# Last stage of a four-layer kernel: rows scattered before their affine, and another order of the routing steps

## The chip, the cores and the metric

The kernel runs on one core of a Trainium2 chip. The metric is the device time of one execution in microseconds. Before the change the median of three runs was 1690.9 us (1688.8 to 1695.48).

## What is computed

Four layers follow one another on `x` (2 x 1024 rows of 256). The change touches only the last one, a mixture of eight experts between two layer norms. Cut to that:

```python
def _ln(x, g, b, eps=1e-05):
    mu = jnp.mean(x, -1, keepdims=True)
    v = jnp.mean((x - mu) ** 2, -1, keepdims=True)
    return (x - mu) * jax.lax.rsqrt(v + eps) * g + b

def _moe(x, wg, w1, b1, w2, b2):          # S = 2048 rows, E = 8, cap = 256
    gates = jax.nn.softmax(xf @ wg, axis=-1)
    idx = jnp.argmax(gates, axis=-1)
    mask1 = jax.nn.one_hot(idx, E)
    loc = jnp.sum((jnp.cumsum(mask1, 0) - 1.0) * mask1, -1)
    keep = loc < cap
    slot = jnp.where(keep, idx * cap + loc, E * cap)
    disp = jnp.zeros((E * cap, D)).at[slot].set(xf, mode='drop').reshape(E, cap, D)
    h = jnp.einsum('ecd,edf->ecf', disp, w1) + b1[:, None, :]
    y = (jnp.einsum('ecf,efd->ecd', h, w2) + b2[:, None, :]).reshape(E * cap, D)
    return jnp.where(keep[:, None], gate_val[:, None] * y[slot], 0.0)

y1 = _ln(x + _mha(x, ...), ln1_g, ln1_b)
y2 = _ln(y1 + _moe(y1, ...), ln2_g, ln2_b)
```

There is no nonlinearity between `w1` and `w2`, so the kernel uses their product (`g.w12`, 256 x 256 for each expert) and one offset row for each expert (`g.c12`).

## The kernel before, in words

The last stage is the function `tail`. Its 2048 rows are 16 tiles of 128, taken as eight pairs. Each engine has its own instruction stream, written out by hand, and semaphores tie the streams together; there is no planner. The stage has three parts.

**Routing.** For each pair p, TensorE makes the sums before the norm in PSUM (`products`). VectorE takes their statistics (`measure`), ScalarE the root (`deviation`), and VectorE writes the normalised rows (`scale`). TensorE turns these (`turn`), ScalarE applies gain and offset on the way to `y1f` (`keep_rows`), TensorE makes the eight logits (`logits`) and ScalarE copies them (`keep_logits`). VectorE picks the expert (`choose`), TensorE counts the rows ahead (`count` on TensorE) and VectorE works out the slot (`count` on VectorE). All eight pairs pass through one loop on each engine, and a step of a later kind stands at a distance: in iteration i VectorE measures pair i, chooses for pair i-3, scales pair i and counts pair i-4. PSUM has two buffers for the sums (`ps_n`); products of pair i wait until pair i-2 is scaled.

GpSimd makes the residual rows in the same loop: two tensor operations for each pair, gain and then offset, from `nrm` (two buffers) into `y1t`. From iteration 4 on it also issues the indirect DMAs that scatter the two tiles of pair i-4 from `y1t` to `slot_rows` in HBM, which SyncE has zeroed.

**Experts.** When all 16 scatters have landed, SyncE loads the slots in four pieces into `held`. For each expert TensorE turns 256 slots (`turn_slots`), ScalarE copies them to `turned`, TensorE multiplies, VectorE adds the offset row (`outputs`) and SyncE stores the result. After each copy ScalarE also makes a piece of the last residual (`outcome`).

**Gather and second norm.** GpSimd issues 16 indirect DMAs back into `held` once all results are stored. VectorE adds `y1t` and measures (`mix`), ScalarE normalises, TensorE turns, VectorE finishes (`give`), SyncE stores.

Here `then` settles after each of its operations: VectorE waits for the result before the next one starts. A line such as `dve.wait_ge(y1t_step, 2 * (p - 1))` waits on a semaphore count.

Of the kernel before, what the change touches and what calls it, by code (L numbers as in the profile page):

```python
# [13 lines left out]
ALU = mybir.AluOpType  # L14
# [2005 lines left out]
def tail(nc, a, g, out):  # L2020

    with Stage(nc, "tail") as st:
# [65 lines left out]
        def _(dve):  # L2088
# [19 lines left out]
            def scale(p):  # L2108
                dve.wait_ge(sd_done, p + 1)
                then(dve.reciprocal(sd[:, 0, 2 * p:2 * p + 2], sd[:, 0, 2 * p:2 * p + 2]))  # L2110
                if p >= 2:
                    dve.wait_ge(t_ready, p - 1)
                    dve.wait_ge(y1t_step, 2 * (p - 1))
                s.did(normalize(2 * p, nrm[p % 2][:, 0, :], ps_n[p % 2][:, 0, :]))
                normalize(2 * p + 1, nrm[p % 2][:, 1, :], ps_n[p % 2][:, 1, :]).then_inc(n_done, 1)
                dve.wait_ge(n_done, p + 1)
# [106 lines left out]
        def _(pool):  # L2223
# [10 lines left out]
            pool.wait_ge(presets, 6)  # L2234
            pool.wait_ge(spread_done, 1)
            for i in range(NPAIR + 4):
                if i < NPAIR:
                    y = y1t[:, 2 * i:2 * i + 2, :]
                    pool.wait_ge(n_done, i + 1)
                    pool.tensor_tensor(y, nrm[i % 2][:], affine[:, 0, :].unsqueeze(1).to_broadcast([P, 2, D]), ALU.mult).then_inc(y1t_step, 1)  # L2240
                    pool.wait_ge(y1t_step, 2 * i + 1)
                    pool.tensor_tensor(y, y, affine[:, 1, :].unsqueeze(1).to_broadcast([P, 2, D]), ALU.add).then_inc(y1t_step, 1)
                if i == 4:
                    pool.wait_ge(rows_written, 16 * 2)
                if i >= 4:
                    p = i - 4
                    pool.wait_ge(vstep, marks["slot", p])
                    pool.wait_ge(y1t_step, 2 * (p + 1))
                    for t in range(2 * p, 2 * p + 2):
                        pool.indirect_dma_start(g.slot_rows, bass.IndirectOffsetOnAxis(ap=slot[:, t:t + 1], axis=0),  # L2250
                                                y1t[:, t, :], None).then_inc(g.row_load[0], 16)
            pool.wait_ge(g.row_load[0], scattered)
            pool.wait_ge(vstep, marks["row"])
# [9 lines left out]
        def _(pe):  # L2263
# [12 lines left out]
            def turn(p):  # L2276
# [42 lines left out]
            def expert(e):  # L2319
                pe.wait_ge(y1f_done, NPAIR * C + e + 1)  # L2320
# [25 lines left out]
            for i in range(NPAIR + 4):  # L2346
                if i < NPAIR:
                    products(i)
                if 0 <= i - 2 < NPAIR:
                    turn(i - 2)  # L2350
                if 0 <= i - 3 < NPAIR:
                    if i == 3:
                        pe.wait_ge(spread_done, 1)
                    logits(i - 3)
                if 0 <= i - 4 < NPAIR:
                    count(i - 4)
# [10 lines left out]
        def _(act):  # L2367
# [221 lines left out]
```

## Time and profile before

| | us |
|---|---|
| median of three runs | 1690.9 |
| the profiled execution | 1689.8 |
| its span | 1688.1 |
| TensorE busy | 1504.5 |
| VectorE busy | 1080.0 |
| ScalarE busy | 446.1 |
| GpSimd busy | 462.6 |
| mean granted TensorE clock | 0.94 of full speed |

The span runs from the first to the last instruction of one execution; start and end around it take the other 1.7 us. The last stage begins at about 1554 us and takes the last 134 us. PE is TensorE, DVE is VectorE, ACT is ScalarE, POOL is GpSimd, and SPq is the queue of SyncE. A busy TensorE is not necessarily a TensorE at its peak, since the ends of pipelined matmuls are modelled.

### The profile page before, as it was taken

What the parts mean: (1) busy time and instruction counts of PE and PEld (TensorE: products, weight loads), DVE (VectorE), ACT (ScalarE), POOL (GpSimd) and SP (SyncE); (2) the same over time, 40 slices, a digit from 0 to 9 for tenths busy, and PEclk for the clock granted to TensorE, in tenths of its full rate; (3) what the DMA queues carried; (4) which work ended last, traced back from release to release, by engine and by line L of the source; (5) the groups of instructions that cost most, each with busy time, mean ns of one, the idle gap of its engine ahead of it and who ended that gap; (6) DMA issues with size and microseconds to landing.
All of it is one profiled execution on the core that took longest, in us unless ns stands there. A gap on an engine that the chain in (4) does not pass through costs nothing. (4 is left out here: it accounts for less than half of the span.)

```text
span 1688.1 us, 26682 instructions
## 1 busy us (share of the span) xinstructions
PE 1504.5 (89%) x10586; PEld 924.9 (55%) x10586; DVE 1080.0 (64%) x3225; ACT 446.1 (26%) x687; POOL 462.6 (27%) x392
## 2 busy tenths in 40 slices
PE   7989789999999996898888889899998999698882
PEld 3447678888888884443333333344444558344761
DVE  1539898687877662487785667644783498423745
ACT  2332111111111000232333323321112477413232
POOL 0002323231415405066666575400000000000623
PEclk9999899999999997899999899999999999899865
DMA  8900000000000016365557664420142027000235
GB/s 355 228 9 1 2 2 8 2 9 2 9 2 9 3 32 224 141 196 165 172 164 266 192 208 142 131 112 1 37 163 63 14 83 240 0 7 1 70 124 107
DMA packets 86991, 155.92 MB, mean 92 GB/s; under 512 B 42075, under 2 KB 56532, under 8 KB 84308
## 3 DMA queue, kind: packets, MB, share of 16 engines
q1 hardware_dynamic: 64852, 82.91, 14.9%
q0 software_dynamic: 22016, 71.32, 14.2%
q8 instruction: 83, 1.36, 0.3%
q14 instruction: 40, 0.33, 0.1%
HBM read 141.62 MB, written 16.78 MB: 94 GB/s over the span
## 5 line engine op out<-in xcount | busy, mean ns | idle before, releaser
L514 PE MATMUL peer_ps_h<-all_x,layer_down 128*128 128x256 f32 x768 | 180.0, 388 | 0.0
L650 POOL TENSOR_TENSOR peer_bm<-peer_bm,peer_slots 128x512 f32<-128x512 f32 x36 | 109.0, 3028 | 244.7 <-DVE peer_bm L746 244.7
L1420 PE MATMUL skills_acc<-skills_hid,skills_w 128*128 128x512 f32 x256 | 129.7, 632 | 37.0 <-DVE skills_hid L1153 26.7
L514 PEld LDWEIGHTS peer_ps_h<-all_x,layer_down 128*128 128x128 f32 x768 | 144.3, 192 | 21.7 <-issue 1.9
L553 PE MATMUL peer_ps_o<-peer_hg,layer_up 128*128 128x256 f32 x640 | 142.3, 380 | 0.4 <-DVE peer_hg L778 0.4
L553 PEld LDWEIGHTS peer_ps_o<-peer_hg,layer_up 128*128 128x128 f32 x640 | 120.5, 190 | 20.4 <-issue 3.3
L595 ACT ACTIVATE peer_hg<-peer_ps_h 128x512 f32<-128x512 f32 x96 | 57.3, 597 | 274.6 <-PE peer_ps_h L514 274.6
L1473 PE MATMUL skills_ps_g<-all_x,skills_w 128*128 128x512 f32 x256 | 121.7, 598 | 0.0
L1473 PE MATMUL skills_ps_u<-all_x,skills_w 128*128 128x512 f32 x256 | 120.3, 592 | 0.0
L1420 PEld LDWEIGHTS skills_acc<-skills_hid,skills_w 128*128 128x128 f32 x256 | 50.2, 200 | 104.9 <-issue 65.0
L1487 ACT ACTIVATE skills_act_g<-skills_ps_g 128x512 f32<-128x512 f32 x96 | 56.3, 597 | 194.1 <-PE skills_ps_g L1473 170.3
L810 POOL DMA_INDIRECT layer_qw<-expert_rows,all_route x88 | 88.3, 1004 | 64.1 <-DVE layers_y L1231 37.1
L1153 DVE SCALAR_TENSOR_TENSOR skills_hid<-skills_ps_u,all_pair_w,skills_act_g 128x512 f32<-128x512 f32 x64 | 48.0, 750 | 84.2 <-ACT skills_act_g L1487 30.3
L778 DVE TENSOR_TENSOR peer_hg<-peer_ps_w,peer_hg 128x1024 f32<-128x1024 f32 x48 | 58.7, 1222 | 61.7 <-PE peer_ps_w L529 61.6
L810 POOL DMA_INDIRECT layer_w<-expert_rows,all_route x88 | 86.7, 985 | 37.8 <-issue 27.4
L810 POOL DMA_INDIRECT four_ring<-expert_rows,all_route x80 | 79.7, 996 | 51.9 <-issue 26.2
L650 POOL TENSOR_TENSOR all_route<-all_route,peer_slots 128x512 f32<-128x512 f32 x12 | 36.3, 3028 | 189.6 <-DVE all_route L746 189.6
L529 PE MATMUL peer_ps_w<-peer_bm,peer_am 64*64 64x32 f32 x4608 | 77.9, 224 | 9.1 <-DVE peer_hg L778 7.6
L1719 PE MATMUL quant_ps_m<-layers_y,layer_qw 128*128 128x512 f32 x192 | 84.1, 593 | 2.0 <-DVE layers_y L1626 2.0
L529 PEld LDWEIGHTS peer_ps_w<-peer_bm,peer_am 64*64 64x64 f32 x4608 | 73.9, 139 | 21.2 <-issue 21.2
L1473 PEld LDWEIGHTS skills_ps_g<-all_x,skills_w 128*128 128x128 f32 x256 | 49.5, 194 | 62.4 <-issue 62.4
L748 DVE TENSOR_TENSOR peer_am<-all_iota_a,peer_slots 128x2048 f32<-128x2048 f32 x36 | 82.2, 2284 | 0.0
(426 smaller groups left out, 2610.1 us busy)
## 6 DMA issues: line engine op xcount, KB each, us to landing
four_ring<-in_l_w SPq DMA_DIRECT2D x8, 1024.0 KB, 4.9
quant_w<-in_l_w SPq DMA_DIRECT2D x32, 256.0 KB, 4.6
all_early<-in_l_w SPq DMA_DIRECT2D x26, 256.0 KB, 3.8
four_skill<-in_skills SPq DMA_DIRECT2D x2, 3072.0 KB
skills_w<-in_skills SPq DMA_DIRECT2D x2, 3072.0 KB
layer_down<-in_down SPq DMA_DIRECT2D x1, 4096.0 KB, 25.5
layer_up<-in_up SPq DMA_DIRECT2D x1, 4096.0 KB, 35.2
expert_rows<-in_up SPq DMA_DIRECT2D x1, 4096.0 KB, 41.2
```

The costliest lines, as they stand in the source:

```text
L514: mm = pe.matmul(ps_h[group % 2][:, r, :], down[:, c, j * P:(j + 1) * P], g.x[:, c, bass.ds(i * PB, PB)], start=(c == 0), stop=(c == C - 1))
L529: mm = pe.matmul(ps_w[of, z, m, :], am[c % RING][token, m, of], bm[c % RING][token, m, :], start=True, stop=True)
L553: mm = pe.matmul(ps_o[:, c, :], up[:, j, c * P:(c + 1) * P], hg[half][:, j, :], start=(j == 0), stop=(j == NJ - 1))
L595: act.activation(hg[half][:, 2 * group:2 * group + 2, :], ps_h[group % 2][:], ACT.Gelu).then_inc(gelu_done, 1)
L650: pool.tensor_tensor(bm[c % RING][:], bm[c % RING][:], slots[half][:, 2, c * PAIRS:(c + 1) * PAIRS].unsqueeze(2).to_broadcast([P, PAIRS, WJ]),
L748: dve.tensor_tensor(am[c % RING][:], g.iota_a[:].unsqueeze(1).to_broadcast([P, PAIRS, P]), slots[half][:, 0, col].unsqueeze(2).to_broadcas ...
L778: dve.tensor_tensor(acts, ps_w[:].rearrange("p z m j -> p z j m"), acts, ALU.mult).then_inc(p_done, 1)
L810: pool.indirect_dma_start(to[:, k, :], None, g.table, bass.IndirectOffsetOnAxis(ap=g.eid[:, n // per, at:at + 1], axis=0)).then_inc(g.row_ ...
L1420: mm = pe.matmul(acc[q % 2][c][:], w_down[s][:, m, c * P:(c + 1) * P], hid[j % 4][:], start=(s == 0 and m == 0), stop=(s == 2 and m == M2 ...
L1473: mm = pe.matmul(bank[:], weight[:, c, m * P:(m + 1) * P], g.x[:, c, q * BLK:(q + 1) * BLK], start=(c == 0), stop=(c == C - 1))
L1487: act.activation(act_g[j % 2][:], ps_g[j % 2][:], ACT.Gelu_apprx_tanh).then_inc(gelu_done, 1)
L1719: mm = pe.matmul(ps_m[n % n_ring][:], wt[z][:, c, m * P:(m + 1) * P], g.y[:, c, q * BLK:(q + 1) * BLK], start=(c == 0), stop=(c == C - 1))
```

## The change

Four things are changed, all in `tail`.

- VectorE writes the normalised rows straight into `y1t`. TensorE turns them from there, and GpSimd scatters them from there without gain and offset.
- Gain and offset are applied later and twice. On the turned slots, ScalarE does it with two half-size activations in place of one copy. On the residual rows, GpSimd does it with the same 16 tensor operations, which now stand behind the 16 scatters.
- `mix` waits for the residual rows.
- The loop is one iteration shorter. The distances are 1, 2 and 3 in place of 2, 3 and 4, and the order within an iteration is another on VectorE, TensorE and ScalarE.

```diff
-                if p >= 2:
-                    dve.wait_ge(t_ready, p - 1)
-                    dve.wait_ge(y1t_step, 2 * (p - 1))
-                s.did(normalize(2 * p, nrm[p % 2][:, 0, :], ps_n[p % 2][:, 0, :]))
+                s.did(normalize(2 * p, y1t[:, 2 * p, :], ps_n[p % 2][:, 0, :]))
...
             def mix(p):
                 dve.wait_ge(g.row_load[p % NRING], landed(p))
+                dve.wait_ge(y1t_step, 2 * (p + 1))
...
-            for i in range(NPAIR + 4):
+            for i in range(NPAIR + 3):
                 if i < NPAIR:
                     measure(i)
+                if 0 <= i - 2 < NPAIR:
+                    choose(i - 2)
+                if i == 3:
+                    dve.wait_ge(presets, 5)
                 if 0 <= i - 3 < NPAIR:
-                    choose(i - 3)
+                    count(i - 3)
                 if i < NPAIR:
                     scale(i)
-                if i == 4:
-                    dve.wait_ge(presets, 5)
-                if 0 <= i - 4 < NPAIR:
-                    count(i - 4)
...
             pool.wait_ge(presets, 6)
+            pool.wait_ge(rows_written, 16 * 2)
+            for p in range(NPAIR):
+                pool.wait_ge(n_done, p + 1)
+                pool.wait_ge(vstep, marks["slot", p])
+                for t in range(2 * p, 2 * p + 2):
+                    pool.indirect_dma_start(g.slot_rows, ...y1t[:, t, :], None).then_inc(g.row_load[0], 16)
             pool.wait_ge(spread_done, 1)
...
+            pool.wait_ge(t_ready, NPAIR)
             pool.wait_ge(g.row_load[0], scattered)
+            for p in range(NPAIR):
+                y = y1t[:, 2 * p:2 * p + 2, :]
+                pool.tensor_tensor(y, y, affine[:, 0, :]..., ALU.mult).then_inc(y1t_step, 1)
+                pool.wait_ge(y1t_step, 2 * p + 1)
+                pool.tensor_tensor(y, y, affine[:, 1, :]..., ALU.add).then_inc(y1t_step, 1)
...
-            for i in range(NPAIR + 3):
+            for i in range(NPAIR + 2):
                 if i % 2 == 0 and i // 2 + 1 < NBLK:
                     residual(i // 2 + 1)
+                if 0 <= i - 2 < NPAIR:
+                    keep_logits(i - 2)
                 if i < NPAIR:
                     deviation(i)
-                if 0 <= i - 2 < NPAIR:
-                    keep_rows(i - 2)
-                if 0 <= i - 3 < NPAIR:
-                    keep_logits(i - 3)
+                if 0 <= i - 1 < NPAIR:
+                    keep_rows(i - 1)
...
-                act.activation(turned[e % 2][:], ps_t[e % 2][:], ACT.Copy).then_inc(y1f_done, 1)
+                for c in range(C):
+                    act.activation(turned[e % 2][:, c, :], ps_t[e % 2][:, c, :], ACT.Identity,
+                                   bias=..., scale=...).then_inc(y1f_done, 1)
```

One full iteration of VectorE's routing loop, in the kernel before (`tail_g` are the largest logits, `tail_ps_n` the sums, `tail_spot` and `tail_slot` the slot numbers):

```order
L2099 BN_STATS tail_stat<-tail_ps_n 128x6 x2
L2102 BN_AGGR tail_mv<-tail_stat 128x2 x2
L2121 MAX tail_g<-tail_logit 128x8 x2
L2122 MAX_INDEX tail_gi<-tail_g,tail_logit 128x8 x2
L2123 CAST tail_gif<-tail_gi 128x2
L2124 TENSOR_TENSOR tail_hot<-all_iota_a,tail_gif 128x16
L2110 RECIPROCAL tail_sd<-tail_sd 128x2
L2106 TENSOR_SCALAR tail_nrm<-tail_ps_n,tail_mv,tail_sd 128x256 x2
L2131 TENSOR_TENSOR tail_before<-tail_free,tail_before 128x8 x2
L2133 TENSOR_TENSOR tail_keep<-tail_free,tail_before 128x16
```

The same iteration in the changed kernel, from the end of choosing to the scaled rows:

```order
L2121 TENSOR_TENSOR tail_hot<-all_iota_a,tail_gif 128x16
L2128 TENSOR_TENSOR tail_before<-tail_free,tail_before 128x8 x2
L2130 TENSOR_TENSOR tail_keep<-tail_free,tail_before 128x16
L2132 SCALAR_TENSOR_TENSOR tail_hot<-tail_keep,tail_hot 128x16
L2134 TENSOR_TENSOR tail_spot<-tail_keep,tail_spot 128x16
L2135 TENSOR_TENSOR tail_spot<-tail_spot,tail_hot 128x16
L2136 TENSOR_REDUCE tail_slot_f<-tail_spot 128x2
L2137 TENSOR_TENSOR tail_slot_f<-tail_slot_f,tail_own 128x2
L2138 CAST tail_slot<-tail_slot_f 128x2
L2110 RECIPROCAL tail_sd<-tail_sd 128x2
L2106 TENSOR_SCALAR tail_y1t<-tail_ps_n,tail_mv,tail_sd 128x256 x2
```

The slot arithmetic has moved in front of the reciprocal and the scaling, and it belongs to a pair one iteration younger.

GpSimd's stream where it meets the scatters, before:

```order
L2240 TENSOR_TENSOR tail_y1t<-tail_nrm,tail_affine 128x512
L2242 TENSOR_TENSOR tail_y1t<-tail_y1t,tail_affine 128x512
L2250 DMA slot_rows<-tail_y1t,tail_slot 4096x256 x2
L2240 TENSOR_TENSOR tail_y1t<-tail_nrm,tail_affine 128x512
L2242 TENSOR_TENSOR tail_y1t<-tail_y1t,tail_affine 128x512
L2250 DMA slot_rows<-tail_y1t,tail_slot 4096x256 x10
L2259 DMA tail_held<-out_rows,tail_row 128x256 x16
```

and in the changed kernel (the two tensor operations repeat eight times):

```order
L2231 MEMSET tail_held 128x4096
L2238 DMA slot_rows<-tail_y1t,tail_slot 4096x256 x16
L2245 TENSOR_TENSOR tail_y1t<-tail_y1t,tail_affine 128x512
L2247 TENSOR_TENSOR tail_y1t<-tail_y1t,tail_affine 128x512
L2245 TENSOR_TENSOR tail_y1t<-tail_y1t,tail_affine 128x512
```

All 16 tensor operations have moved from the routing loop to the stretch between the last scatter and the first gather.

## Rows read from the trace of the kernel before

**Rows 1.** The page's first line.

```profile
span 1688.1 us, 26682 instructions
```

**Rows 2.** The chain that ended last, by time: start us, us, what.

```profile
1620.81 3.81 DMA tail_held<-slot_rows
...
1624.67 1.97 PE tail_ps_t L2316 x8
...
1649.00 0.99 POOL tail_held L2259
```

**Rows 3.** Timeline of VectorE, routing: start us, us, instruction [idle before <-releaser].

```profile
1566.67 0.76 DVE L2099 BATCH_NORM_STATS2 tail_stat<-tail_ps_n 128x6 f32<-128x256 f32 x2 [0.42 <-PE tail_ps_n L2273]
...
1575.04 0.76 DVE L2099 BATCH_NORM_STATS2 tail_stat<-tail_ps_n 128x6 f32<-128x256 f32 x2
...
1582.83 0.76 DVE L2099 BATCH_NORM_STATS2 tail_stat<-tail_ps_n 128x6 f32<-128x256 f32 x2
...
1585.21 0.24 DVE L2121 MAX8 tail_g<-tail_logit 128x8 f32<-128x8 f32 x2 [1.34 <-ACT tail_logit L2390]
...
1587.56 0.37 DVE L2131 TENSOR_TENSOR tail_before<-tail_free,tail_before 128x8 f32<-128x8 f32 x2
...
1589.03 1.22 DVE L2138 TENSOR_TENSOR tail_spot<-tail_spot,tail_hot 128x16 f32<-128x16 f32 x1
...
1590.76 0.75 DVE L2099 BATCH_NORM_STATS2 tail_stat<-tail_ps_n 128x6 f32<-128x256 f32 x2
...
1606.32 0.23 DVE L2121 MAX8 tail_g<-tail_logit 128x8 f32<-128x8 f32 x2
...
1609.90 0.36 DVE L2131 TENSOR_TENSOR tail_before<-tail_free,tail_before 128x8 f32<-128x8 f32 x2
...
1611.49 0.23 DVE L2121 MAX8 tail_g<-tail_logit 128x8 f32<-128x8 f32 x2
...
1616.63 0.17 DVE L2141 CAST tail_slot<-tail_slot_f 128x2 uint32<-128x2 f32 x1 [0.76 <-DVE tail_slot_f L2140]
```

**Rows 4.** Timeline of ScalarE, one routing iteration and the first slot copy.

```profile
1583.90 0.29 ACT L2379 ACTIVATE tail_sd<-tail_mv,all_eps 128x2 f32<-128x2 f32 x1 [6.51 <-DVE tail_mv L2102]
1584.10 1.00 ACT L2385 ACTIVATE tail_y1f<-tail_ps_t,layer_cols 128x256 f32<-128x256 f32 x2
...
1625.82 0.60 ACT L2413 ACTIVATE tail_o<-tail_ps_t 128x512 f32<-128x512 f32 x1 [4.27 <-PE tail_ps_t L2316]
```

**Rows 5.** Timeline of GpSimd: one pair's residual rows, and the last scatter.

```profile
1587.61 1.26 POOL L2240 TENSOR_TENSOR tail_y1t<-tail_nrm,tail_affine 128x512 f32<-128x512 f32 x1 [1.38 <-DVE tail_nrm L2106]
1588.95 1.26 POOL L2242 TENSOR_TENSOR tail_y1t<-tail_y1t,tail_affine 128x512 f32<-128x512 f32 x1
...
1618.34 0.96 POOL L2250 DMA_INDIRECT slot_rows<-tail_y1t,tail_slot  x1 [0.30 <-issue]
```

**Rows 6.** Timeline of TensorE, routing.

```profile
1575.15 1.10 PE L2271 MATMUL tail_ps_n<-layer_w_out,layer_o 128*128 128x256 f32 x4
...
1577.84 0.60 PE L2282 MATMUL tail_ps_t<-all_ident,tail_nrm 128*128 128x128 f32 x4
...
1587.67 2.04 PE L2271 MATMUL tail_ps_n<-layer_w_out,layer_o 128*128 128x256 f32 x4 [0.16 <-DVE tail_nrm L2106]
...
1592.92 0.79 PE L2282 MATMUL tail_ps_t<-all_ident,tail_nrm 128*128 128x128 f32 x4
...
1600.86 1.88 PE L2291 MATMUL tail_free<-layer_wg,tail_y1f 128*128 128x8 f32 x8 [4.85 <-ACT tail_y1f L2385]
```

**Rows 7.** Windows: stretch, us, busy PE, PEld, DVE, ACT, POOL; clock, DMA share, GB/s.

```profile
1575.00:1578.00 3.00, 3.00 (x21) 2.79 (x21) 1.55 (x10) 1.28 (x4) 2.54 (x2) 1.00 0.01 3
...
1587.00:1590.00 3.00, 2.84 (x10) 2.40 (x10) 2.83 (x8) 0.00 (x0) 2.31 (x2) 0.50 0.08 23
```

**Rows 8.** Groups of instructions: busy us, mean ns | idle before, releasers.

```profile
L2158 DVE TENSOR_TENSOR tail_y1f<-tail_ps_n,tail_c_rows 128x512 f32<-128x512 f32 x8 | 5.5, 692 | 22.2 <-PE tail_ps_n L2327 22.2
...
L650 POOL TENSOR_TENSOR peer_bm<-peer_bm,peer_slots 128x512 f32<-128x512 f32 x36 | 109.0, 3028 | 244.7 <-DVE peer_bm L746 244.7
```

More of the change, by code:

```diff
@@ L2110, in scale @@
                 then(dve.reciprocal(sd[:, 0, 2 * p:2 * p + 2], sd[:, 0, 2 * p:2 * p + 2]))
-                if p >= 2:
-                    dve.wait_ge(t_ready, p - 1)
-                    dve.wait_ge(y1t_step, 2 * (p - 1))
-                s.did(normalize(2 * p, nrm[p % 2][:, 0, :], ps_n[p % 2][:, 0, :]))
-                normalize(2 * p + 1, nrm[p % 2][:, 1, :], ps_n[p % 2][:, 1, :]).then_inc(n_done, 1)
+                s.did(normalize(2 * p, y1t[:, 2 * p, :], ps_n[p % 2][:, 0, :]))
+                normalize(2 * p + 1, y1t[:, 2 * p + 1, :], ps_n[p % 2][:, 1, :]).then_inc(n_done, 1)
                 dve.wait_ge(n_done, p + 1)
@@ L2234, in _ @@
             pool.wait_ge(presets, 6)
-            pool.wait_ge(spread_done, 1)
[L2236 to L2251, printed above, removed]
-            pool.wait_ge(g.row_load[0], scattered)
+            pool.wait_ge(rows_written, 16 * 2)
[3 more added lines that the diff above has]
+                for t in range(2 * p, 2 * p + 2):
+                    pool.indirect_dma_start(g.slot_rows, bass.IndirectOffsetOnAxis(ap=slot[:, t:t + 1], axis=0),
+                                            y1t[:, t, :], None).then_inc(g.row_load[0], 16)
+            pool.wait_ge(spread_done, 1)
+            pool.wait_ge(t_ready, NPAIR)
+            pool.wait_ge(g.row_load[0], scattered)
+            for p in range(NPAIR):
+                y = y1t[:, 2 * p:2 * p + 2, :]
+                pool.tensor_tensor(y, y, affine[:, 0, :].unsqueeze(1).to_broadcast([P, 2, D]), ALU.mult).then_inc(y1t_step, 1)
+                pool.wait_ge(y1t_step, 2 * p + 1)
+                pool.tensor_tensor(y, y, affine[:, 1, :].unsqueeze(1).to_broadcast([P, 2, D]), ALU.add).then_inc(y1t_step, 1)
             pool.wait_ge(vstep, marks["row"])
@@ L2281, in turn @@
                     for i in range(2):
-                        mm = pe.transpose(ps_t[p % 2][:, c, i * P:(i + 1) * P], nrm[p % 2][:, i, c * P:(c + 1) * P], g.ident[:])
+                        mm = pe.transpose(ps_t[p % 2][:, c, i * P:(i + 1) * P], y1t[:, 2 * p + i, c * P:(c + 1) * P], g.ident[:])
                 mm.then_inc(t_ready, 1)
@@ L2319, in expert @@
             def expert(e):
-                pe.wait_ge(y1f_done, NPAIR * C + e + 1)
+                pe.wait_ge(y1f_done, (NPAIR + e + 1) * C)
                 if e < 2:
@@ L2345, in _ @@
             mm.then_inc(spread, 1)
-            for i in range(NPAIR + 4):
+            for i in range(NPAIR + 3):
                 if i < NPAIR:
@@ L2349, in _ @@
                 if 0 <= i - 2 < NPAIR:
-                    turn(i - 2)
+                    if i == 2:
+                        pe.wait_ge(spread_done, 1)
+                    logits(i - 2)
                 if 0 <= i - 3 < NPAIR:
[L2352 to L2356, printed above, removed]
+                    count(i - 3)
+                if 0 <= i - 1 < NPAIR:
+                    turn(i - 1)
             spread_offsets()
@@ L2412, in _ @@
                     act.wait_ge(n_ready, NPAIR + e - 1)
-                act.activation(turned[e % 2][:], ps_t[e % 2][:], ACT.Copy).then_inc(y1f_done, 1)
+                for c in range(C):
+                    act.activation(turned[e % 2][:, c, :], ps_t[e % 2][:, c, :], ACT.Identity,
+                                   bias=g.cols[:, 2 * C + c:2 * C + c + 1], scale=g.cols[:, C + c:C + c + 1]).then_inc(y1f_done, 1)
                 outcome(e // C, e % C)
```

3 lines of the change are left out of this document (2 added, 1 removed).

## The prediction, made before the changed kernel was run

> **What bounds the kernel now.** The first line of the page gives a span of 1688.1 us [rows 1]; the profiled execution took 1689.8 us, so 1.7 us lie around it, and it stands 1.1 us under the median of the three runs. Only the last stage changes, so what is ahead of it is left as it is, and I read the chain of waits of that stage next. The reader is to see two hinges there. SyncE loads the slots at 1620.81, the instant the last scatter has landed, and the next link is TensorE at 1624.67; GpSimd's first gather starts at 1649.00 [rows 2]. Everything before 1620.81 is one question: what makes the last scatter late? The 28.2 us between the hinges and the 39 us behind the second are a fixed train in which each step waits for the one before.
>
> For the first question I read VectorE's timeline in the routing loop. Iterations start at 1575.04, 1582.83, 1590.76, and the last full one ends at 1606.32; from there only choosing and counting remain, until the last slot number is written at 1616.63 + 0.17 = 1616.80 [rows 3]. The last scatter follows at 1618.34 [rows 5]. So VectorE sets the pace: four iterations take 1606.32 - 1575.04 = 31.28 us, 7.8 each. Two things inside such an iteration are not work. VectorE is idle 1.34 us before it can choose, released by the copied logits [rows 3]: ScalarE first waits for the statistics that VectorE has just made (1583.90), then keeps rows for 1.00 us from 1584.10, and only then copies logits that have long been ready [rows 4]. And the slot arithmetic takes 1590.76 - 1587.56 = 3.20 us here, while the same eight steps later take 1611.49 - 1609.90 = 1.59 us; one of its operations on 128x16 elements took 1.22 us from 1589.03 and ended at 1590.25 [rows 3], when GpSimd's tensor operation from 1588.95 ended, at 1590.21 [rows 5]. VectorE's small operation stood still behind GpSimd's.
>
> The Trainium skill, "SBUF — State Buffer", section "SBUF: two separate sides", says that a VectorE operation with two SBUF inputs and a GpSimd operation that reads SBUF exclude each other for the whole instruction. The row agrees.
>
> **The change, part by part.**
>
> *An iteration of VectorE.* Measuring takes 1583.90 - 1582.83 = 1.07 us, choosing and scaling together 1587.56 - 1585.21 = 2.35, counting without GpSimd beside it 1.59 [rows 3, 4]: 5.0 us in place of 7.8. The idle 1.34 goes because ScalarE now copies logits ahead of the deviation, provided that they are ready. TensorE's work for one iteration at full clock is one turn, the products (1577.84 - 1575.15 = 2.7 us [rows 6]), logits and count, by the rows about 0.5 + 2.7 + 0.9 + 0.5 = 4.6 us, under 5.0. Followed from the scaling of a pair: turn 0.5, rows kept after the next deviation at +1.3 to +2.3, products of a later pair until +3.2, logits until +4.1, copied at +4.3. VectorE asks for them at 5.0 + 1.07 = +6.1. So 1.8 us are to spare and 5.0 holds.
>
> *Start of the loop.* The third pair is measured at 1566.67 before [rows 3]. Now the first turn (0.4 to 0.5 us) stands ahead of its products, so it is 1567.1. Then come measure, choose and scale (3.4 us), 1570.5; the next products end 0.5 us after that, and a full iteration of 5.0 ends at 1576.1. Before, this point was at 1575.04: 1.0 us lost, since choosing and counting begin one iteration earlier.
>
> *Four full iterations.* 31.28 against 4 x 5.0 = 20.0: 11.3 us gained.
>
> *Drain.* Before, 1616.80 - 1606.32 = 10.5 us. Now choose and count (2.7), then the last pair. Its turn, kept rows, logits and copy follow the last scaling: with TensorE at half clock about 1.0 + 1.1 + 1.9 + 0.2 = 4.2 us (1.88 for the logits in [rows 6]), so that VectorE waits until +4.2, chooses (1.1), and counts twice (3.2): 8.4 us. Gain 2.1. At full clock it would be about 7.0. I take half clock, since TensorE has no products left there and the rows of the drain before show it.
>
> *Scatters.* GpSimd now only issues them, one in 0.30 + 0.96 = 1.26 us [rows 5], 2.5 for a pair, less than an iteration. Only in the drain are two pairs ready 1.6 us apart: 0.9 us lost. Landing behind the last one is as before. Taking the normalise from `nrm` to `y1t` costs nothing, as shape, source and engine stay, and the two waits in it go. The last scatter has landed 1.0 - 11.3 - 2.1 + 0.9 = 11.5 us earlier, at 1609.3. What is late next is the offset products on TensorE, which stand behind the last count (about 1602.4) and ahead of the turned slots: sixteen of 256 columns at 2.04 / 4 = 0.5 us each [rows 6] end before 1610.6, and the slots arrive at 1609.3 + 3.8 = 1613.1. Still hidden.
>
> *Turned slots.* One copy of 0.60 us becomes two halves of 1.00 us together [rows 4]. Later experts have a whole matmul of the previous expert as cover. The first has none: 0.4 us lost.
>
> *Residual rows.* Sixteen GpSimd operations at 1588.95 - 1587.61 = 1.34 us [rows 5] are 21.4 us. They start when the scatters have landed, and the gathers queue behind them on GpSimd, 28.2 us later [rows 2]. They are hidden with 6.8 us to spare. VectorE works beside them only on `outputs`, eight of 0.69 us with one operand in PSUM [rows 8]. If each of these held GpSimd up in full it would be 5.5 us more, 26.9 in all, still hidden; from the other side it is nothing. I take nothing, since VectorE's operation on PSUM at 1587.56 took 0.37 us beside GpSimd's at 1587.61 and 0.36 at 1609.90 with none [rows 3, 5]. The added wait in `mix` is then met long before. By the skill's rule, too, an operation with one SBUF input takes no lock.
>
> *Sum.* 11.5 - 0.4 = 11.1 us gained. 1689.8 - 11.1 = 1678.7; from the median it is 1679.8. I say 1679.3.
>
> **Rivals.**
>
> *A: the clock falls inside the loop and TensorE becomes the bound.* At 1575 to 1578 TensorE is busy without a break and the granted clock is 1.00 (2.4 GHz); at 1587 to 1590 it is 0.50 (1.2 GHz) [rows 7], after the waits that VectorE's slow iterations gave it. There the products took 1592.92 - 1587.67 = 5.25 us and logits 1.88 [rows 6]; with a turn of 1.0 and counts of 1.0 an iteration costs TensorE 9.1 us. For it: the new loop leaves TensorE some 10% idle in small waits. Against it: before it stood idle far more when the clock fell, and the shorter loop takes these waits away. Each iteration caught costs 9.1 - 5.0 = 4.1, the first 1.8 less. With two caught it is 6.4 us: 1679.3 + 6.4 = 1685.7. The Trainium skill, "TensorE: Matmul & The Clock Gate", section "HAM oscillation — how this bites in real kernels", warns that a matmul loop with a wait in each turn can fall back to half rate every time; the rows show one such fall.
>
> *B: GpSimd's sixteen operations outlast the experts, and the kernel gets slower.* Another 128x512 operation of GpSimd took 3.03 us on average [rows 8]. At that price they take 16 x 3.1 = 49.6 us, the gathers start 49.6 - 28.2 - 0.4 = 21.0 us late, and the time is 1679.3 + 21.0 = 1700.3. It decides from (28.2 + 0.4) / 16 = 1.8 us each. Against it: the 3.03 are taken beside large VectorE operations on SBUF alone, and no such operation runs between the hinges. The same length on the same tiles was 1.26.
>
> *C: the earlier routing is given back.* Something not seen in the rows, such as late slot loads or a colder clock at the experts, holds the second hinge. The clock there is 0.50 at the start in both kernels, and TensorE pauses for the slots in both. If three experts more ran at half clock, some 2 us each, it would cost 6 us: 1685.3.
>
> **How the numbers follow.** Forecast 0.74, A 0.13, B 0.04, C 0.09. A measurement of this kernel tells about 0.5% from no change, 8.5 us. Below 1682.4 lie the forecast and a part of A with one iteration caught: faster 0.78. The rest of A and C: same 0.17. B, and A through five iterations (which would cost 18.7), make slower 0.05. The low end is the drain at full clock (1.4 us better), no loss at the start (1.0) and some scatter of the median: 1675.5. The high end is A with two iterations: 1685.7.
>
> **What would show it.** VectorE's iterations start 5.0 us apart and L2135, the former L2138, takes 0.17 us. No idle time before the largest logits but for the last pair. The granted clock stays 1.00 up to the last products. SyncE's slot load starts at about 1609, the first gather at about 1638. GpSimd's sixteen operations end about 7 us before that gather. The forecast is wrong if iterations are longer than 6 us, or if the first gather follows directly on GpSimd's last tensor operation.

## The result, and the profile after

The changed kernel ran in 1681.15 us (median of six runs, 1676.21 to 1682.39), the kernel before in 1689.97 us in the same comparison (six runs, 1686.9 to 1695.48). The ratio is 0.9933, with a 95% interval of 0.9915 to 0.9952. The prediction said 1679.3 us, or 0.9931 of the 1690.9 us known then. In a later comparison, on a chip where everything is 4% shorter, the same two kernels gave 0.9925 (0.9911 to 0.9939).

The page and one line of VectorE's timeline (start us, duration us, instruction) give the length of the last stage. I take it from VectorE's `memset` of the counters to the end of the span. Of the changed kernel:

```profile
span 1680.7 us, 26688 instructions
```

```profile
1559.47 0.07 DVE L2197 MEMSET tail_before<- 128x8 f32 x1
```

The same line of the kernel before, which the rows above did not hold:

```profile
1555.31 0.07 DVE L2199 MEMSET tail_before<- 128x8 f32 x1
```

So the stage was 1688.1 - 1555.31 = 132.8 us long [rows 1] and is 1680.7 - 1559.47 = 121.2 us: 11.6 us shorter. The span fell by only 7.4 us, since this execution came to the stage 4.2 us later, though nothing ahead of it differs. The stage is the better ruler for what follows: its start varied by 16 us over the profiles below that are near 1690 us long, while the length of the changed kernel's stage repeated within 0.5 us.

VectorE's timeline of the changed kernel, one full iteration, the next one's start, and the drain:

```profile
1580.13 0.76 DVE L2099 BATCH_NORM_STATS2 tail_stat<-tail_ps_n 128x6 f32<-128x256 f32 x2
...
1584.85 0.76 DVE L2099 BATCH_NORM_STATS2 tail_stat<-tail_ps_n 128x6 f32<-128x256 f32 x2
1585.65 0.25 DVE L2102 BATCH_NORM_AGGREGATE tail_mv<-tail_stat 128x2 f32<-128x6 f32 x2
1585.81 0.21 DVE L2118 MAX8 tail_g<-tail_logit 128x8 f32<-128x8 f32 x2
...
1587.69 0.17 DVE L2135 TENSOR_TENSOR tail_spot<-tail_spot,tail_hot 128x16 f32<-128x16 f32 x1
...
1599.10 0.24 DVE L2118 MAX8 tail_g<-tail_logit 128x8 f32<-128x8 f32 x2
...
1603.48 0.24 DVE L2118 MAX8 tail_g<-tail_logit 128x8 f32<-128x8 f32 x2 [1.69 <-ACT tail_logit L2385]
...
1607.54 0.27 DVE L2138 CAST tail_slot<-tail_slot_f 128x2 uint32<-128x2 f32 x1
```

An iteration takes 1584.85 - 1580.13 = 4.7 us, where it was 7.8 [rows 3]. The largest logits follow the statistics without a pause, and L2135, the operation that stood at 1.22 us, takes 0.17. The one wait left is 1.69 us for the logits of the last pair. ScalarE has copied the logits in time, here by 1585.00, when VectorE asks for them at 1585.81:

```profile
1584.82 0.18 ACT L2385 ACTIVATE tail_logit<-tail_free 128x16 f32<-128x16 f32 x1 [2.39 <-PE tail_free L2286]
```

GpSimd's timeline and SyncE's load, with the second hinge:

```profile
1606.88 0.95 POOL L2238 DMA_INDIRECT slot_rows<-tail_y1t,tail_slot  x1 [2.12 <-DVE tail_hot L2132]
1608.14 0.96 POOL L2238 DMA_INDIRECT slot_rows<-tail_y1t,tail_slot  x1 [0.30 <-DVE tail_row_f L2145]
1609.41 0.96 POOL L2238 DMA_INDIRECT slot_rows<-tail_y1t,tail_slot  x1 [0.30 <-issue]
1610.67 0.96 POOL L2238 DMA_INDIRECT slot_rows<-tail_y1t,tail_slot  x1 [0.30 <-issue]
1613.24 1.26 POOL L2245 TENSOR_TENSOR tail_y1t<-tail_y1t,tail_affine 128x512 f32<-128x512 f32 x1 [1.61 <-DMA slot_rows<-tail_y1t,tail_slot]
...
1632.60 1.28 POOL L2247 TENSOR_TENSOR tail_y1t<-tail_y1t,tail_affine 128x512 f32<-128x512 f32 x1
1640.98 1.02 POOL L2254 DMA_INDIRECT tail_held<-out_rows,tail_row  x1 [7.10 <-DMA out_rows<-tail_y1f]
```

```profile
1613.14 2.02 SPq L2435 DMA_DIRECT2D tail_held<-slot_rows  x4
```

The sixteen tensor operations end at 1633.88, and GpSimd is then idle for 7.10 us until the last result has landed. That is the cover that the residual rows have. The first gather starts at 1640.98, was 1649.00 [rows 2]; against the start of the stage it comes 12.2 us earlier.

### The profile page after: what moved, and what is told of

Same layout as the page of the kernel before. It is cut to its first block and busy times, and to the rows that moved or that the text cites. A ratio compares the mean times of both kernels' runs of the same rounds, so it can differ in the third digit from the quotient of the medians.

```text
span 1680.7 us, 26688 instructions
## 1 busy us (share of the span) xinstructions
PE 1502.3 (89%) x10586; PEld 920.4 (55%) x10586; DVE 1072.3 (64%) x3225; ACT 450.2 (27%) x695; POOL 462.2 (27%) x392
## 5 line engine op out<-in xcount | busy, mean ns | idle before, releaser
L553 PEld LDWEIGHTS peer_ps_o<-peer_hg,layer_up 128*128 128x128 f32 x640 | 120.5, 190 | 20.3 <-issue 3.3
L595 ACT ACTIVATE peer_hg<-peer_ps_h 128x512 f32<-128x512 f32 x96 | 57.3, 597 | 273.8 <-PE peer_ps_h L514 273.8
L1473 PE MATMUL skills_ps_u<-all_x,skills_w 128*128 128x512 f32 x256 | 120.3, 592 | 0.0
L778 DVE TENSOR_TENSOR peer_hg<-peer_ps_w,peer_hg 128x1024 f32<-128x1024 f32 x48 | 58.7, 1223 | 62.4 <-PE peer_ps_w L529 62.3
L529 PE MATMUL peer_ps_w<-peer_bm,peer_am 64*64 64x32 f32 x4608 | 78.2, 224 | 11.1 <-DVE peer_hg L778 9.3
L1473 PEld LDWEIGHTS skills_ps_u<-all_x,skills_w 128*128 128x128 f32 x256 | 48.7, 190 | 61.8 <-issue 61.3
## 6 DMA issues: line engine op xcount, KB each, us to landing
skills_w<-in_skills SPq DMA_DIRECT2D x2, 3072.0 KB, 10.5
```

The lines of the kernel that those rows point to most:

```text
L529: mm = pe.matmul(ps_w[of, z, m, :], am[c % RING][token, m, of], bm[c % RING][token, m, :], start=True, stop=True)
L553: mm = pe.matmul(ps_o[:, c, :], up[:, j, c * P:(c + 1) * P], hg[half][:, j, :], start=(j == 0), stop=(j == NJ - 1))
L595: act.activation(hg[half][:, 2 * group:2 * group + 2, :], ps_h[group % 2][:], ACT.Gelu).then_inc(gelu_done, 1)
L778: dve.tensor_tensor(acts, ps_w[:].rearrange("p z m j -> p z j m"), acts, ALU.mult).then_inc(p_done, 1)
L1473: mm = pe.matmul(bank[:], weight[:, c, m * P:(m + 1) * P], g.x[:, c, q * BLK:(q + 1) * BLK], start=(c == 0), stop=(c == C - 1))
```

## The experiments

Twelve more profiles follow, one of them of the changed kernel again: the first four on one chip, the next four on another, the last four on a third. Six of them (logits last, plain copy, no residual affine, 16 more on GpSimd, idle matmuls, wide offsets) have one execution each, so for those only the stage in the profile is read. In the table the times are us from the start of the stage in the profiled execution. "Iteration 4" is the start of the fifth statistics, with which the full iterations begin; "pace" is the mean of the last three steps from one start of statistics to the next.

| kernel | iteration 4 | pace | slots ready | slot load | first turn | first gather | length |
|---|---|---|---|---|---|---|---|
| before | 19.7 | 7.8 | 61.5 | 65.5 | 69.4 | 93.7 | 132.8 |
| changed | 20.7 | 4.7 | 48.3 | 53.7 | 57.6 | 81.5 | 121.2 |
| deferral only | 19.3 | 6.2 | 55.5 | 60.0 | 63.9 | 88.2 | 128.1 |
| order only | 21.8 | 5.7 | 53.4 | 58.7 | 62.6 | 85.4 | 125.2 |
| changed, logits copied last | 22.4 | 6.2 | 56.4 | 61.7 | 65.6 | 90.6 | 130.2 |
| changed, one plain copy | 20.6 | 4.7 | 48.3 | 53.7 | 57.5 | 81.4 | 121.3 |
| changed, no residual affine | 20.3 | 4.7 | 48.0 | 53.4 | 57.3 | 81.0 | 120.7 |
| changed, 16 more on GpSimd | 20.6 | 4.7 | 48.3 | 53.7 | 57.5 | 94.3 | 134.4 |
| changed, drain reordered | 20.3 | 4.7 | 47.6 | 52.1 | 56.0 | 80.7 | 120.5 |
| changed, idle matmuls | 20.6 | 4.7 | 48.3 | 53.7 | 57.5 | 80.3 | 120.3 |
| changed, run again | 20.3 | 4.7 | 48.0 | 53.3 | 57.3 | 81.1 | 120.7 |
| drain and idle matmuls | 20.3 | 4.7 | 47.6 | 52.1 | 56.0 | 80.5 | 120.6 |
| changed, wide offsets | 20.4 | 4.7 | 48.1 | 53.4 | 57.3 | 81.1 | 120.9 |
| all three | 20.3 | 4.7 | 47.6 | 52.1 | 55.9 | 79.8 | 119.7 |

There are two kinds of start, 5.6 to 5.7 or 5.9 to 6.0 us until the first statistics. They go with the clock of the first products: in the last us before the stage the granted clock was 1.00 for the early kind (1554 to 1555 us in the kernel before) and 0.50 for the late kind (1558 to 1559 us in the changed kernel). The late kind shifts everything behind by 0.3 to 0.4 us. A length is best compared with the changed kernel of the same start: 121.2 for the late kind, 120.7 for the early one. The kernel before had the early start and the first profile of the changed kernel the late one, so like for like the change is worth 132.8 - 120.7 = 12.1 us in the stage.

### Deferral alone

```diff
 kernel before, and in it:
-  normalize(...) -> nrm; GpSimd makes y1t in the loop
+  normalize(...) -> y1t; GpSimd scatters raw rows, makes the residual rows behind the scatters
-  ACT.Copy of the turned slots
+  two ACT.Identity with scale and bias
   order and distances of the routing steps: as before
```

> The kernel before with only the deferral: rows scattered raw, gain and offset later, loop order and distances as before. Length of the last stage means from VectorE's memset of `before` to the end of the span: 132.8 us before (1555.3 to 1688.1), 121.2 changed (1559.5 to 1680.7). Theory 1 (two separate costs in an iteration: 1.6 us of VectorE standing behind GpSimd's tensor operations, and 1.34 us idle for the logits): iterations become 7.8 - 1.5 = 6.3 us, the idle 1.34 stays, stage 127 to 128. Rival (the order of the steps is what counts, the stalls are absorbed by waiting): iterations stay at 7.5 or more, stage 132 or more.

Ratio to the kernel before 0.9957 (0.9929 to 0.9985). The stage is 128.1 us long, the pace 6.2 us. VectorE's timeline shows that the idle time stayed and the stalls went:

```profile
1589.27 0.24 DVE L2118 MAX8 tail_g<-tail_logit 128x8 f32<-128x8 f32 x2 [1.35 <-ACT tail_logit L2385]
...
1592.38 0.18 DVE L2135 TENSOR_TENSOR tail_spot<-tail_spot,tail_hot 128x16 f32<-128x16 f32 x1
```

The first theory holds: standing behind GpSimd's operations was a cost of its own, 1.6 us in each iteration.

### Order alone

```diff
 changed kernel, and in it:
-  normalize(...) -> y1t; residual rows behind the scatters
+  normalize(...) -> nrm; GpSimd makes y1t of pair i and scatters pair i - 3 in one loop
-  two ACT.Identity on the turned slots
+  ACT.Copy
   order and distances of the routing steps: new
```

> The kernel before with only the new order and distances; GpSimd still makes the residual rows in the loop, and the copies are plain. Theory 1: the idle 1.34 goes, the stalls behind GpSimd stay, iterations 6.3 us, stage 127 to 128, so that this and the deferral alone add up to about 11.6. Rival (either edit alone gives nearly all): stage under 124. Second rival: GpSimd is the bound with two tensor operations and two scatters for a pair (5.1 us), which would show as VectorE waiting on it.

Ratio 0.9968 (0.9943 to 0.9992); the interval overlaps that of the deferral alone, and only the stage, read from one profile each, tells them apart. It is 125.2 us long, 2 us shorter than expected, at a pace of 5.7 in place of 6.3. VectorE's timeline, and GpSimd's beside it:

```profile
1590.27 0.16 DVE L2122 FIND_INDEX8 tail_gi<-tail_g,tail_logit 128x8 uint32<-128x8 f32 x1
1590.46 1.08 DVE L2123 CAST tail_gif<-tail_gi 128x2 f32<-128x2 uint32 x1
...
1592.57 0.17 DVE L2138 TENSOR_TENSOR tail_spot<-tail_spot,tail_hot 128x16 f32<-128x16 f32 x1
```

```profile
1590.25 1.27 POOL L2242 TENSOR_TENSOR tail_y1t<-tail_y1t,tail_affine 128x512 f32<-128x512 f32 x1
```

The stall is there, but only one of 0.9 us in an iteration: the cast ends at 1591.54, GpSimd's operation at 1591.52. In the other order the slot arithmetic falls between GpSimd's operations. So what GpSimd's presence costs depends on what VectorE is about to do when one of its operations starts, and the expectation of 1.6 us was carried over without asking that. The second rival is out: VectorE waited for GpSimd nowhere in the loop. The edits apart save 4.7 and 7.6 us, which adds to 12.3, and together they save 11.6 (each against the 132.8 before, all with the late start): nearly additive, and neither gives all. The ratios of whole executions stand in the other order, within their intervals.

### The logits' place on ScalarE

```diff
 changed kernel, ScalarE's loop:
-  keep_logits(i - 2); deviation(i); keep_rows(i - 1)
+  deviation(i); keep_rows(i - 1); keep_logits(i - 2)
```

> The changed kernel with one edit: ScalarE copies the logits last in its iteration, behind deviation and kept rows. Theory 1: VectorE is idle about 1.34 us in each full iteration again, iterations 4.75 + 1.3 = 6.1 us, stage longer by 6 to 8 us (127 to 129). Rival (the idle time went because the iteration has other work to fill it): stage within 1 us of 121.2.

The stage is 130.2 us long, 9.5 more than the changed kernel of the same start and over the 6 to 8 expected. The slots are ready 8.4 us later; another 1.2 us lies between first turn and first gather, where the first expert took 3.78 us, wholly at half clock. The pace is 6.2 us, and VectorE is idle for the logits again:

```profile
1588.45 0.24 DVE L2118 MAX8 tail_g<-tail_logit 128x8 f32<-128x8 f32 x2 [1.35 <-ACT tail_logit L2385]
```

ScalarE's timeline is that of the kernel before [rows 4] again, with the logits at the end:

```profile
1587.14 0.30 ACT L2374 ACTIVATE tail_sd<-tail_mv,all_eps 128x2 f32<-128x2 f32 x1 [4.89 <-DVE tail_mv L2102]
1587.34 1.00 ACT L2380 ACTIVATE tail_y1f<-tail_ps_t,layer_cols 128x256 f32<-128x256 f32 x2
1588.24 0.18 ACT L2385 ACTIVATE tail_logit<-tail_free 128x16 f32<-128x16 f32 x1
```

One copy of 0.18 us, placed behind 1.2 us of other work, costs more than the deferral gains. With it the shorter distances are worth nothing: the stage is even 2 us longer than with the deferral alone.

### The copy of the turned slots

```diff
 changed kernel:
-  for c in range(C): act.activation(turned[e % 2][:, c, :], ps_t[e % 2][:, c, :], ACT.Identity, bias=..., scale=...)
+  act.activation(turned[e % 2][:], ps_t[e % 2][:], ACT.Copy)
```

> The changed kernel with one copy of the turned slots in place of two activations; gain and offset of the expert's input are left out. Theory 1: only the first expert lacks cover, so the stage is 0.4 us shorter (120.8). Rival: each expert pays, 8 x 0.4 = 3.2 us shorter.

The stage is 121.3 us, against 121.2. The later experts are hidden, so the rival is out. The length does not show the 0.4 us of the first expert, but TensorE's timeline does, changed kernel first and plain copy second:

```profile
1617.04 1.97 PE L2311 MATMUL tail_ps_t<-all_ident,tail_held 128*128 128x128 f32 x8 [4.30 <-DMA tail_held<-slot_rows]
1619.27 3.23 PE L2322 MATMUL tail_ps_n<-layer_w,tail_o 128*128 128x256 f32 x8 [0.26 <-ACT tail_o L2409]
```

```profile
1609.39 1.97 PE L2311 MATMUL tail_ps_t<-all_ident,tail_held 128*128 128x128 f32 x8 [4.25 <-DMA tail_held<-slot_rows]
1611.20 3.46 PE L2322 MATMUL tail_ps_n<-layer_w,tail_o 128*128 128x256 f32 x8
```

From the first turn to the first expert it is 2.23 us with the halves and 1.81 with the plain copy: the 0.4 us are paid. But in both kernels the clock rose at the same time, in the 1 us windows that start 62.0 us behind the start of the stage (mean clock 0.83 and 0.85). The expert that began 0.4 us later had less of its work at half clock and was 0.23 us shorter, and by the first gather 0.1 us was left.

### Residual rows left out, and doubled

```diff
 changed kernel, behind the scatters:
-  8 x (mult by gain, add offset) on y1t         (left out)
 or
+  16 x mult on scratch, ahead of them           (doubled)
```

> The changed kernel without the sixteen tensor operations of GpSimd behind the scatters; gain and offset of the residual rows are left out. Theory 1 (hidden, with about 7 us to spare, and nothing else slowed by them): stage 121.2, within 0.3. Rival (they slow VectorE or the loads beside them): 1 us or more shorter, to be seen between slot load and first gather.

> The changed kernel with sixteen more tensor operations of the same size on GpSimd, on scratch, ahead of the sixteen. Theory 1: 16 x 1.28 = 20.5 us more against 7.1 us to spare; the first gather comes 13.4 us later and the stage is 134.6, slower than the kernel before. Rival B of the prediction (GpSimd slows itself beside VectorE's outputs): the operations are longer than 1.28 us and the stage over 136.

Without them the stage is 120.7 us, as the changed kernel of the same start. Slot load to first gather took 27.6 us against 27.8: they slow nothing beside them. With sixteen more it is 134.4 us, 0.2 from the expectation. GpSimd's timeline of the doubled kernel:

```profile
1615.44 19.70 POOL L2249 TENSOR_TENSOR tail_nrm<-tail_nrm,tail_affine 128x512 f32<-128x512 f32 x16 [1.60 <-DMA slot_rows<-tail_y1t,tail_slot]
...
1654.52 1.26 POOL L2255 TENSOR_TENSOR tail_y1t<-tail_y1t,tail_affine 128x512 f32<-128x512 f32 x1
1655.93 1.02 POOL L2262 DMA_INDIRECT tail_held<-out_rows,tail_row  x1 [0.15 <-issue]
```

The first gather now follows directly on the last tensor operation. They took 1.23 us (19.70 / 16) and 1.26 us each, those beside VectorE's outputs too, not 3.03 [rows 8]: rival B's mechanism does not occur here, but its arithmetic (time beyond the cover is paid in full) does. The 36 operations of rows 8 all lie between 3.025 and 3.031 us, which speaks for a cost of their own form and not for waiting; no run tests that.

### The drain

```diff
 changed kernel, iteration 9:
-  TensorE: logits(7), count(6)     VectorE: choose(7), count(6)
+  TensorE: count(6), logits(7)     VectorE: count(6), choose(7)
```

> The changed kernel with another order in the drain only: the count of pair 6 goes ahead of the last pair's logits on TensorE and ahead of its choosing on VectorE. The 1.69 us in which VectorE is idle for the last logits then hold a count. Slot 6 is ready 2.7 us earlier, so that GpSimd's last four scatters are no longer bunched: last scatter issued 1.9 us earlier, stage 119.3. Rival (the last pair's chain decides, the bunching is absorbed): 0.7 us or less.

The slot load comes 1.2 us earlier than in the changed kernel of the same start, the first gather 0.4 and the end 0.2 (120.5 against 120.7). In the run, the ratio to the kernel before is 0.9932 (0.9915 to 0.9948), no different from the changed kernel. The bunching did go (the last pair's scatters start 0.75 us after its slots are written), but most of the gain was lost behind the load. TensorE's timeline:

```profile
1613.63 1.97 PE L2313 MATMUL tail_ps_t<-all_ident,tail_held 128*128 128x128 f32 x8 [3.00 <-DMA tail_held<-slot_rows]
1615.85 3.78 PE L2324 MATMUL tail_ps_n<-layer_w,tail_o 128*128 128x256 f32 x8 [0.26 <-ACT tail_o L2413]
```

The first expert took 3.78 us at half clock, where that of the changed kernel took 3.15 with the same start and 3.23 with the late one. The first turns began 1.3 us earlier, but the clock did not rise earlier. Windows of 1 us, 61 us behind the start of the stage, of the changed kernel of the same start and of this one:

```profile
1547.47:1548.47 1.00, 1.00 (x4) 0.82 (x3) 0.00 (x0) 0.57 (x1) 1.00 (x2) 0.56 0.01 4
```

```profile
1618.67:1619.67 1.00, 1.00 (x5) 0.71 (x4) 0.00 (x0) 0.00 (x0) 0.92 (x2) 0.51 0.00 0
```

In the window before, the clock is 0.50 in both, in the one behind 1.00. So most of the time won ahead of the experts was spent at half clock in the first of them.

### The clock ahead of the experts

Four kernels followed that up. Idle matmuls are matmuls whose result nobody reads:

```diff
             spread_offsets()
+            pe.wait_ge(vstep, marks["counted", NPAIR - 1])
+            for n in range(4):
+                pe.matmul(free[2][:, 0:D], g.ident[:], g.w12[:, 0, n % E3, :], start=True, stop=True)
             turn_slots(0)
```

> The changed kernel with four matmuls of 128x256 into unused PSUM, in TensorE's pause of 4.3 us before the turned slots. At half clock they take 1.0 us each, so they fit. Theory: the granted clock answers to work on all 128 rows, so it rises earlier; the first turns take 0.9 in place of 2.0 us and the first expert 1.7 in place of 3.2; the stage is 1.5 to 2.6 us shorter. Rival: the clock does not answer in that time, 0; or they end after the slots have landed, 0.5 us longer.

The stage is 120.3 us, 0.9 less than with the same start in the changed kernel; the expectation was 1.5 to 2.6. TensorE's timeline: the four matmuls (eight records, since each fp32 matmul leaves two) at half clock, then the first turns in 1.73 us and the first expert in 1.99:

```profile
1609.49 3.78 PE L2355 MATMUL tail_free<-layer_w,all_ident 128*128 128x256 f32 x8
1613.83 1.73 PE L2311 MATMUL tail_ps_t<-all_ident,tail_held 128*128 128x128 f32 x8 [0.55 <-DMA tail_held<-slot_rows]
1616.06 1.99 PE L2322 MATMUL tail_ps_n<-layer_w,tail_o 128*128 128x256 f32 x8 [0.49 <-ACT tail_o L2412]
```

On the chip of the later comparison, the changed kernel again:

> The changed kernel once more, to be compared with the next runs on one chip. All theories: stage 121.2, within 0.5; the start of the stage (1559.5 in the profiled execution, 1555.3 in that of the kernel before) moves by several us between executions without cause in the change, since nothing ahead of it differs.

Its stage is 120.7 us, 1608.7 us in all against 1622.33 before. Then both edits together, three idle matmuls:

> The drain order and three idle matmuls of 128x256 together. The drain order alone left 3.0 us of pause before the turned slots and gave back 0.8 us, since the first expert then ran wholly at half clock; three matmuls at 0.9 us fill that pause. Theory (the clock answers to work on 128 rows shortly ahead): both gains add, stage 121.2 - 1.2 - 1.2 = 118.8. Rival (the rise comes at times that the pause does not set): 120.

The stage is 120.6 us: the theory fell. The three matmuls filled the pause at half clock, the first expert took 3.78 us, and nothing was gained:

```profile
1538.66 2.93 PE L2359 MATMUL tail_free<-layer_w,all_ident 128*128 128x256 f32 x6
1541.72 1.97 PE L2313 MATMUL tail_ps_t<-all_ident,tail_held 128*128 128x128 f32 x8
1543.94 3.78 PE L2324 MATMUL tail_ps_n<-layer_w,tail_o 128*128 128x256 f32 x8 [0.26 <-ACT tail_o L2416]
```

The rows agree with the rival: the clock rose 61.9 us behind the start of the stage (mean 0.53 in the 1 us window from 61.0), as in the changed kernel of this start and in the reordered drain, with the pause filled or not. In the kernel with four idle matmuls and the late start it rose at 58.9, and at 62.3 in the changed kernel of that start. What sets these times is not shown, so it stays open why four idle matmuls brought the rise forward and three did not. The median was 1607.82 us with a ratio of 0.9911 (0.9898 to 0.9924); the interval overlaps that of the changed kernel beside it, 0.9925 (0.9911 to 0.9939), so that no difference is shown. Then the offset products over all rows, alone and with the rest:

```diff
-  pe.matmul(ps_b[k][:, i, :], g.ident[0:E3, e:e + 1].to_broadcast([E3, P]), g.c12[:], ...)
+  pe.matmul(ps_b[k][:, i, :], g.ident[:, e:e + 1].to_broadcast([P, P]), c128[:], ...)   # zeros below row 8
```

> The changed kernel, with the sixteen offset products made over 128 rows (offsets padded with zeros) in place of 8 rows. They are busy for 7.2 us at half clock throughout in every run so far. Theory (matmuls over 8 rows count for little with the clock): the granted clock rises within the sixteen, they end in 5 to 6 us, and may leave the clock up for the first turns, 0 to 2 us shorter. Rival (rows do not matter, or zeros do not count): 7.2 us at 0.50 again and the same stage.

> Drain order, wide offsets and four idle matmuls together. If wide offsets lift the clock, TensorE is at full clock up to near the turned slots and the first expert takes 1.7 us: stage 121.2 - 1.2 - 2.5 = 117.5. Rival (the clock falls again in what is left of the pause): as the drain order with idle matmuls, 118.8 to 120.

The first half of the theory holds. (The sixteen products are sixteen records of eight matmuls.) Windows of the changed kernel on that chip (stretch, us, busy PE, PEld, DVE, ACT, POOL, then clock, DMA share, GB/s), and of the wide offsets:

```profile
1531.47:1534.47 3.00, 3.00 (x9) 2.52 (x10) 2.56 (x17) 0.00 (x0) 0.93 (x1) 0.50 0.12 44
1534.47:1537.47 3.00, 3.00 (x8) 2.32 (x7) 0.93 (x5) 1.39 (x3) 2.09 (x4) 0.50 0.24 87
1537.47:1540.47 3.00, 1.93 (x5) 1.00 (x3) 0.00 (x0) 1.19 (x2) 1.39 (x2) 0.50 0.24 87
```

```profile
1532.81:1535.81 3.00, 3.00 (x9) 2.37 (x8) 1.00 (x6) 1.39 (x3) 2.08 (x4) 0.50 0.24 87
1535.81:1538.81 3.00, 1.29 (x5) 0.78 (x3) 0.00 (x0) 1.19 (x2) 1.39 (x2) 0.91 0.24 87
1538.81:1541.81 3.00, 0.00 (x0) 0.00 (x0) 0.00 (x0) 0.00 (x0) 2.92 (x3) 0.66 0.76 243
```

Over 8 rows the products are busy for 7.2 us and the clock stays at 0.50; over 128 rows it rises before they end, and they end after 6.6 us. But TensorE then pauses for 5.0 us, the clock is back at 0.50 for the first turns, and the stage is 120.9 us: no gain. With drain order, wide offsets and four idle matmuls the stage is 119.7 us, the shortest of all, though 2.2 us over the expectation. After a pause of 2.0 us the first turns ran at full clock, but the clock fell again within the first expert:

```profile
1546.60 1.09 PE L2318 MATMUL tail_ps_t<-all_ident,tail_held 128*128 128x128 f32 x8 [2.00 <-DMA tail_held<-slot_rows]
1548.36 3.30 PE L2329 MATMUL tail_ps_n<-layer_w,tail_o 128*128 128x256 f32 x8 [0.67 <-ACT tail_o L2421]
```

The median of that kernel was 1610.21 us (0.9922, 0.9909 to 0.9936), so 1 us in the stage doesn't show in the whole. No version is shown to beat the changed kernel.

## Why the prediction was right, point by point

| step | predicted | measured |
|---|---|---|
| iteration 4 starts later | 1.0 | 0.9 (0.6 with the early start, which the kernel before had) |
| an iteration | 5.0 | 4.7 |
| four iterations gain | 11.3 | 31.28 - 18.97 = 12.3 |
| drain gains | 2.1 | 10.5 - 8.7 = 1.8 |
| bunched scatters cost | 0.9 | 5.3 - 4.0 = 1.3 |
| two halves of the copy cost | 0.4 | 0.4 (first turn to first expert 1.80 us before, 2.23 after) |
| from first expert to first gather | 0 | 0.8 shorter (22.53 to 21.71) |
| from first gather to the end | 0 | 0.6 longer (39.1 to 39.7) |
| sum | 11.1 gained | 11.6 gained |

The prediction was right in its mechanism and in the size of most terms. That the sum comes within 0.5 us is in part luck, since the errors have both signs: 1.0 us too little for the iterations, against 0.3 too much for the drain, 0.4 too little cost for the scatters and 0.6 behind the gathers. The 0.8 us between first expert and first gather were not foreseen at all.

*The first expert.* It took 3.78 us before and 3.23 after. In both kernels it began at half clock, but in the changed one the clock rose 4.8 us behind the first turn, in the kernel before 6.2. No run shows what sets the time of the rise, so the 0.8 us can't be credited to the change; without them the gain is 10.8 us.

*What bounds.* That the last slot number sets the hinge, and VectorE's iteration the slot number, held. Each of the two costs named in an iteration came back when its edit was undone: the idle time in the kernel with the logits copied last, the stalls, in part, in the kernel with the order alone.

*An iteration.* It was sized 0.3 us too long. The 1.07 us for measuring ran to the start of ScalarE, while VectorE's own next operation starts 0.96 us after the statistics, and choosing and scaling take 2.2. The 1.8 us to spare for the logits were 0.5 to 1.4 (1580.65 against 1581.10, 1593.91 against 1595.32). And TensorE, said to be some 10% idle, was busy 24.9 of the 25 us from 1565 to 1590: VectorE waits for nothing and sets the pace, but TensorE has next to nothing to spare, so a shorter iteration could make it the bound. That was not run.

*The drain.* TensorE at half clock was the right choice: its logits for the last pair took 1.88 us, and VectorE was idle 1.69. The last pair's logits came 0.2 us later than worked out. The terms of the prediction for the drain add to 8.5 us, not 8.4; measured are 8.7.

*Scatters.* The price of the bunching was 0.4 us too small. The four scatters ran back to back as said, and landing behind the last took 1613.14 - 1611.63 = 1.5 us, as before. But the first of them began only at 1606.88, 0.75 us after the slots of its pair were written (1606.13), where the last pair before had waited 0.27. The pair ahead waited 0.76 too; why, no run shows.

*Residual rows.* Hidden with 6.8 us to spare was said, 7.10 us of idle time was measured.

*Behind the first gather.* The prediction took this stretch as unchanged, at 39.1 us. It is 39.5 to 40.2 us in every other profile, with either edit alone too. The cause stays open.

*Rival A* did not come about. These windows of the changed kernel show the clock at 1.00 with TensorE busy without a break up to the end of the last products, at 1592.9. It falls 5 us behind them, at about 1597.9, after TensorE has waited 1.66 us for kept rows:

```profile
1590.00:1593.00 3.00, 3.00 (x23) 2.79 (x21) 2.65 (x20) 1.20 (x3) 1.14 (x2) 1.00 0.24 87
1593.00:1596.00 3.00, 1.80 (x15) 1.47 (x14) 2.79 (x16) 0.75 (x3) 1.72 (x2) 1.00 0.12 44
1596.00:1599.00 3.00, 1.64 (x12) 1.53 (x12) 2.69 (x14) 0.82 (x3) 0.47 (x2) 0.82 0.12 44
1599.00:1602.00 3.00, 1.77 (x7) 1.37 (x8) 2.41 (x18) 1.02 (x2) 1.64 (x2) 0.50 0.24 87
```

The Trainium skill, "TensorE: Matmul & The Clock Gate", section "HAM oscillation — how this bites in real kernels", warns of loops that fall back to half rate at each wait. In this loop TensorE had no wait to speak of up to the last products, and the rows show no fall. Behind them, after waits of 0.2 and 1.7 us, they show one, and in the kernel with wide offsets another in the pause of 5.0 us.

*Rival B* was settled by the doubled operations: 1.26 us each, under the 1.8 from which it decides. *Rival C* did not come about between these two kernels; the first expert even gained. Its mechanism exists: over all kernels the first expert takes between 2.0 and 3.8 us, and 0.6 us of what the reordered drain had won went there.

The 8.8 us between the medians are 2.8 less than the stage shows, the 13.6 us of the later comparison 2.0 more. The first interval (0.9915 to 0.9952 is 8 to 14 us) holds 11.6, so the whole kernel and the stage don't contradict each other. Medians of the whole can't tell more: what lies ahead of the stage is the same in both kernels and varies by more than the difference.

## What to carry to other kernels

In a loop that several engines share, ask of each short operation what stands ahead of it on its own in-order engine: here a copy of 0.18 us, which the critical engine waited for, stood behind 1.2 us of work that nobody needed yet, and its place was worth more (9.5 us) than taking 20 us of tensor operations out of the loop (4.7 us, from the kernel before). Work moved off such a loop should go where its engine is idle and the next thing in its queue is far; leaving it out and doubling it measures that cover from both sides. Work that a change brings forward may meet a lower clock: here 1.3 us won ahead of the experts left 0.2 at the end. Where the part ahead of the changed stage varies more than the stage gains, compare the stage and not the span.

## What the runs showed of the hardware

- Small VectorE operations beside a GpSimd tensor operation on SBUF fall into two kinds. In the order-only kernel a cast of 128x2 took 1.08 us and ended with GpSimd's operation, while the search for indices ahead of it, 128x8 from SBUF, took 0.16 us within the same GpSimd operation. The statistics, which read PSUM, took 0.76 us beside GpSimd and without it. The Trainium skill, "SBUF — State Buffer", section "SBUF: two separate sides", names two SBUF inputs or a 2-port mode as the condition. The arithmetic on two SBUF tiles agrees [rows 3, 5]; the search, whose row names two SBUF tiles as well, does not. That a cast of two elements is held up was not expected. The cost was the rest of GpSimd's operation, however small the operation of VectorE.
- The offset products over 8 rows kept TensorE busy for 7.2 us with the clock at 0.50 throughout, in all twelve profiles that have them. The same products over 128 rows, most of them zeros, ended with the clock at full speed, in both kernels that have them.
- The kernel before took 1690 us in one comparison and 1622 us in another, on another chip. In the profiles, the granted clock from 600 to 1200 us was 0.91 to 0.96 in the first and 0.97 to 1.00 in the changed kernel's profile of the other. How much of the 68 us that explains is not shown. The ratio of the two kernels agreed within its intervals.
